# Attention with sixteen heads: the last probability tile of a head joins GpSimd's partial sum by an accumulating transfer instead of by an add

## The chip, the cores and the metric

The kernel runs on one core of a Trainium2 chip. The metric is the device time of one execution in microseconds (us), lower is better. Three runs of the kernel before gave 4175.97, 4178.22 and 4180.62 us.

## What is computed

A transformer block on four sequences of 2048 tokens with 512 channels, all in fp32:

```python
xn = _layernorm(x)
q, k, v = heads of (xn @ q_w.T + q_b) / sqrt(32), xn @ k_w.T + k_b, xn @ v_w.T + v_b   # 16 heads of 32 channels
attn = softmax(q @ k.T)                       # per head 2048 x 2048
ctx = attn @ v
out = x + (ctx @ out_w.T + out_b) + tanh(xn @ weight @ aux_weight1 @ aux_weight2 + bias)
```

With four sequences and sixteen heads there are 64 heads to attend.

## The kernel before

Three stages follow each other: the weights (`build_weights`), the projections (`build_project`) and attention with the output projection (`build_attend`). The first two end near 830 us and the change does not touch them.

**A head in attention.** The scores are held transposed, keys in partitions. A head has 16 tiles (`KT`), each of 128 keys by 2048 queries, that is 128x2048 fp32 or 1 MB. TensorE makes the scores of a tile in four units of 512 queries (`scores`, L942), ScalarE takes the exponential of each unit into the tile (`exps`, L762), and TensorE multiplies the tile with v (`use`, L948) and adds up in `pv_bank`. Between the score units of this head TensorE makes plain scores of a following head (`max_scores`, L926), whose row maxima VectorE takes (L846); that maximum goes into the scores as one more row. TensorE works in pairs of tiles: sixteen score matmuls, then `use` of an earlier pair.

**The denominator.** All 16 tiles of a head also have to be summed over the keys. Elementwise sums of whole tiles are made first, in two places. Tiles 0, 2, 5, 8, 10 and 13 (`CHAINS`) go into `dma_sum`: tile 0 is written there by ScalarE, and the others are added by DMAs that accumulate in SBUF (`join` 1 to 5, L708, issued by GpSimd). The other ten tiles (`POOL_TILES`: 1, 3, 4, 6, 7, 9, 11, 12, 14, 15) are summed in `pool_sum` by nine GpSimd adds (`add` 0 to 8, L697). Then `merge` (L716) adds `pool_sum` onto `dma_sum` by one more accumulating DMA. TensorE multiplies the result with ones (`add_up`, L948 with `dma_sum,ones_att`), ScalarE copies it, VectorE takes the reciprocals in three pieces and GpSimd multiplies (`scale`, L722). Both sums are double-buffered by the head's parity.

**GpSimd's order.** Its instruction stream is written out by hand. In `body(h)`, for i from 0 to 8, it runs `sum_up` of the next head h+1, with the merge of head h behind the first of them and `scale(h)` ahead of the last:

```python
JOIN_AFTER = {1: 2, 3: 3, 5: 4, 7: 5}
# body(h): join1(h+1), add0(h+1), merge(h), add1, join2, add2, add3, join3,
#          add4, add5, join4, add6, add7, join5, scale(h), add8(h+1)
```

A join waits for its tile's exponentials and for the landing of the join before it (`joined`, L702 to L706); join 1 waits also until TensorE has used tile 0. The merge waits for the last add and the last join. All six accumulating DMAs of a head are issued by GpSimd and share one queue, q0.

**TensorE's order.** `add_up(h)` stands behind the score units of tiles 8 and 9 and the use of tiles 6 and 7 of head h+1. It waits for the landing of the merge (`joined`), and everything behind it on TensorE waits with it.

**Buffers.** The probability tiles other than tile 0 rotate through eight buffers (`SLOT`). ScalarE may write a tile when TensorE has used the buffer's former tile and the sum has taken it in: `exps` waits for `pool_added` or for `joined` (L753 to L760). Tile 7 of head h+1 follows tile 15 of head h in its buffer.

Of the kernel before, what the change touches and what calls it, by code (L numbers as in the profile page):

```python
# [8 lines left out]
ALU = mybir.AluOpType  # L9
# [13 lines left out]
DMA = 16  # L23
PRIME = 16


KT = SEQ // P
QT = SEQ // P
QB = SEQ // BLK
ALL_HEADS = BATCH * HEADS  # L30
GROUP = 4
# [3 lines left out]
UNITS = KT * QB  # L35
# [9 lines left out]

CHAINS = [[0, 2, 5, 8, 10, 13]]
MERGE_AFTER = 0
POOL_TILES = [kt for kt in range(KT) if not any(kt in tiles for tiles in CHAINS)]
POOL_ADDS = len(POOL_TILES) - 1
JOINED = len(CHAINS[0]) * DMA  # L50
JOIN_AFTER = {1: 2, 3: 3, 5: 4, 7: 5}
SLOT = {kt: i % 7 for i, kt in enumerate([*range(1, 13), 14, 15])} | {13: 7}
SCALE_ADD = 8
RESULT_TILES = [9, 11]


# [20 lines left out]
def st_place(u):  # L77
    return st_slot(u) % ST_BANKS
# [10 lines left out]
def adds_after(kt):  # L89

    return max(1, POOL_TILES.index(kt))


def tile_before(kt):

    same = [t for t in SLOT if SLOT[t] == SLOT[kt]]
    i = same.index(kt)
    return same[i - 1], int(i == 0)
# [422 lines left out]
def build_attend(nc, dram, out, first):  # L521

    with ExitStack() as own:
        sb = lambda name, shape, dt=F32: own.enter_context(nc.sbuf_tensor(name, shape, dt))
        ps = lambda name, shape: own.enter_context(nc.psum_tensor(name, shape, F32))
        sem = lambda name: own.enter_context(nc.semaphore(name))
# [4 lines left out]
        pool_sum = [sb(f"pool_sum{s}", [P, SEQ]) for s in range(2)]  # L533
# [16 lines left out]
        scores_ready, probs_ready, tile_used = sem("scores_ready"), sem("probs_ready"), sem("tile_used")  # L550
        max_scores_ready, max_scores_read = sem("max_scores_ready"), sem("max_scores_read")
        row_max_ready, turned_ready, max_row_ready = sem("row_max_ready"), sem("max_turned"), sem("max_row_ready")
        join_due, joined = sem("join_due"), [sem("joined0"), sem("joined1")]
        pool_added, sums_ready, recip_ready, context_ready = sem("pool_added"), sem("sums_ready"), sem("recip_ready"), sem("context_ready")
        pv_copied, sums_copied = sem("pv_copied"), sem("sums_copied")
        context_stored = [sem("context_stored0"), sem("context_stored1")]
# [16 lines left out]
        def heads(eng, body, extra=0):  # L573


            with nc.Fori(0, ALL_HEADS // GROUP - 1, engines=[eng.engine], hint_back_edge=True,
                         head_slot={eng.engine: 0}) as i:
                after = [eng.snap(i + 1 + n) for n in range(1 + extra)]
                for r in range(GROUP):
                    body(i * GROUP + r, r, GROUP, *(a * GROUP + (r + 1 - GROUP - n * GROUP) for n, a in enumerate(after)))  # L580
            for r in range(GROUP):
                body(ALL_HEADS - GROUP + r, r, GROUP - 1 - r, *[ALL_HEADS - GROUP + r + 1] * (1 + extra))
# [9 lines left out]
        def tile_at(r, kt):  # L592

            return dma_sum[r % 2] if kt == CHAINS[0][0] else probs[SLOT[kt]]

        def landed(h, j):

            return (h // 2) * JOINED + j * DMA
# [76 lines left out]
        @block.gpsimd  # L675
        def _(pool):
            pool.sem_inc(pool_added, PRIME)
            pool.sem_inc(context_ready, PRIME)
            nc.gpsimd.memset(ident[:], 0.0).then_inc(ident_zero, 1)
            nc.gpsimd.memset(ones[:], 1.0).then_inc(consts_ready, 1)  # L680
            pool.wait_ge(ident_zero, 1)
            nc.gpsimd.affine_select(out=ident[:], in_=ident[:], compare_op=ALU.not_equal, fill=1.0, base=0,
                                    pattern=[[-1, P]], channel_multiplier=1).then_inc(consts_ready, 1)
            for r in range(GROUP):
                pool.wait_ge(consts_ready, 2 + r)
                nc.gpsimd.memset(k_st[r][MROW:MROW + 1, :].bitcast(F32), 1.0).then_inc(consts_ready, 1)

            def add(h, r, i):

                total, kt = pool_sum[r % 2], POOL_TILES[i + 1]  # L690
                if i == 0:
                    pool.wait_ge(sums_ready, PRIME + h - 1)
                pool.wait_ge(probs_ready, PRIME + h * UNITS + QB * (kt + 1))
                one = tile_at(r, POOL_TILES[0]) if i == 0 else total
                if i:
                    pool.wait_ge(pool_added, PRIME + h * POOL_ADDS + i)
                nc.gpsimd.tensor_tensor(total[:], one[:], tile_at(r, kt)[:], ALU.add).then_inc(pool_added, 1)  # L697

            def join(h, r, j):


                pool.wait_ge(probs_ready, PRIME + h * UNITS + QB * (CHAINS[0][j] + 1))  # L702
                if j == 1:
                    pool.wait_ge(tile_used, PRIME + h * KT + CHAINS[0][0] + 1)
                if j > 1 or not (isinstance(h, int) and h < 2):
                    pool.wait_ge(joined[r % 2], landed(h, j - 1))  # L706
                pool.sem_inc(join_due, 1)
                nc.gpsimd.dma_start(dma_sum[r % 2][:], tile_at(r, CHAINS[0][j])[:],  # L708
                                    accum_op=ALU.add).then_inc(joined[r % 2], DMA)

            def merge(h, r):

                pool.wait_ge(pool_added, PRIME + h * POOL_ADDS + POOL_ADDS)
                pool.wait_ge(joined[r % 2], landed(h, len(CHAINS[0]) - 1))
                pool.sem_inc(join_due, 1)
                nc.gpsimd.dma_start(dma_sum[r % 2][:], pool_sum[r % 2][:], accum_op=ALU.add).then_inc(joined[r % 2], DMA)  # L716

            def scale(h, r):
                pool.wait_ge(pv_copied, PRIME + h + 1)
                pool.wait_ge(recip_ready, h * len(RECIPS) + len(RECIPS))  # L720
                pool.wait_ge(context_stored[r % 2], PRIME + (h // 2) * (CTX_DMAS * DMA))
                nc.gpsimd.tensor_tensor(ctx_out[r % 2][:], pv_copy[r % 2][:], ratio[:], ALU.mult).then_inc(context_ready, 1)  # L722

            def sum_up(h, r, i):
                if i == 0:
                    join(h, r, 1)
                add(h, r, i)
                if i in JOIN_AFTER:
                    join(h, r, JOIN_AFTER[i])

            for i in range(POOL_ADDS):
                sum_up(0, 0, i)

            def body(h, r, more, following):
                for i in range(POOL_ADDS):
                    if i == SCALE_ADD:
                        scale(h, r)
                    if more >= 1:
                        sum_up(following, (r + 1) % GROUP, i)
                    if i == MERGE_AFTER:  # L740
                        merge(h, r)

            heads(pool, body)

        @block.scalar
        def _(act):
# [3 lines left out]
            def exps(h, r, kt):  # L750

                for q in range(QB):
                    if q == 0 and kt in SLOT:  # L753
                        old, back = tile_before(kt)
                        act.wait_ge(tile_used, PRIME + h * KT - back * KT + old + 1)
                        if old in POOL_TILES:
                            act.wait_ge(pool_added, PRIME + h * POOL_ADDS - back * POOL_ADDS + adds_after(old))
                        elif old != kt and not (back and isinstance(h, int) and h == 0):
                            before, place = (h - 1, (r + 1) % 2) if back else (h, r % 2)
                            act.wait_ge(joined[place], landed(before, CHAINS[0].index(old)))  # L760
                    act.wait_ge(scores_ready, h * UNITS + kt * QB + q + 1)  # L761
                    nc.scalar.activation(tile_at(r, kt)[:, q * BLK:(q + 1) * BLK],  # L762
                                         st_bank[:, st_place(kt * QB + q)], ACT.Exp,
                                         scale=SCALE).then_inc(probs_ready, 1)
# [24 lines left out]
            for kt in range(CUT):  # L789
                exps(0, 0, kt)  # L790
                if kt in LOAD_AT:
                    load(GROUP - 1, GROUP - 1, LOAD_AT.index(kt))
# [297 lines left out]
```

## Time and profile before

| | |
|---|---|
| Runs | 4175.97, 4178.22, 4180.62 us (median 4178.22) |
| Profiled execution | 4178.57 us, span of the core 4176.8 us |
| TensorE busy | 4086.4 us, 98% |
| GpSimd busy | 3251.6 us, 78% of the whole; 979.66 of 1000 us within attention |
| VectorE, ScalarE busy | 74%, 57% |
| DMA, mean over 16 engines | 0.44 in the projections, 0.82 in attention |
| Granted TensorE clock | 0.99 of full speed |

Busy shares average over stages that have different limits. Attention runs from about 830 to 3990 us. Within it the shares are those of one stretch of 1000 us in the rows below. In the waits, an entry says which instruction waited and what ended the wait. In the timeline, a row is one instruction, or several of one kind merged, with its start, its length and the idle time before it. Times from issue to landing are those of single transfers.

### The profile page before, as it was taken

Reading aid. Unit: us, or ns where it says so; the run is one execution under the profiler, and the core shown is the slowest. Engines: PE = TensorE matmul, PEld = TensorE weight load, DVE = VectorE, ACT = ScalarE, POOL = GpSimd, SP = SyncE. Lnnn points to the kernel's source line nnn. Section 1 sums busy time; section 2 is a strip of 40 time slices with the busy share of each in tenths; the row PEclk is TensorE's granted clock in tenths of the full one; section 3 lists DMA queues with packets and bytes.
Section 4 is the critical chain, followed back from the end, with each engine's and each line's share of the span. In section 5 each row is a group of like instructions: output and inputs, shape, how many; then the busy total and the mean of one; then the engine's idle time right before and its main releaser. Section 6 shows DMA issues by size and latency. Waiting matters only on the chain.

```text
span 4176.8 us, 77708 instructions
## 1 busy us (share of the span) xinstructions
PE 4086.4 (98%) x21216; PEld 2490.0 (60%) x21216; DVE 3110.1 (74%) x5056; ACT 2360.6 (57%) x4517; POOL 3251.6 (78%) x1183
## 2 busy tenths in 40 slices
PE   8999999899999999999999999999999999999989
PEld 6888888655555555555555555555555555555467
DVE  4443334588888888888888888888888888888444
ACT  2221222166666666666666666666666667666621
POOL 1222222279999999999999999999999999999920
PEclk9999999999999999999999999999999999999999
DMA  4444445368788888888888888888888888887777
GB/s 169 163 162 158 151 161 170 132 139 170 166 177 175 179 170 174 171 173 172 175 177 173 175 171 167 172 175 177 176 171 172 173 173 175 176 178 163 167 248 250
DMA packets 246256, 722.11 MB, mean 173 GB/s; under 512 B 87296, under 2 KB 88320, under 8 KB 184448
## 3 DMA queue, kind: packets, MB, share of 16 engines
q0 software_dynamic: 55296, 402.68, 49.8%
q1 hardware_dynamic: 107552, 201.88, 14.2%
q10 hardware_dynamic: 83040, 113.01, 9.7%
q8 instruction: 185, 3.03, 0.3%
q14 instruction: 183, 1.50, 0.1%
HBM read 178.00 MB, written 136.31 MB: 75 GB/s over the span
## 4 chain that ended last, share of the span: by engine, by line
PE 48%; DMA 18%; issue 9%; ACT 3%; POOL 2%; POOLq 0%; DVE 0%; ACTq 0%; SPq 0%; DVEq 0%
PE sm_bank L926 14%; PE st_bank L942 14%; PE pv_bank L948 14%; DMA dma_sum<-pool_sum 10%; DMA dma_sum<-probs 7%; PE sm_bank L235 3%; ACT probs L762 3%; PE sm_bank L948 1%; POOL pool_sum L697 1%; PE st_bank L235 1%; POOL ctx_out L722 1%; POOL dma_sum L708 0%; PE sm_bank L935 0%; ACTq L761 0%; DMA k_stack<-s_k_hi 0%
## 5 line engine op out<-in xcount | busy, mean ns | idle before, releaser
L846 DVE TENSOR_REDUCE part_max<-sm_bank 128x1 f32<-128x512 f32 x4032 | 2450.4, 677 | 413.8 <-PE sm_bank L926 407.4
L697 POOL TENSOR_TENSOR pool_sum<-pool_sum,probs 128x2048 f32<-128x2048 f32 x512 | 2503.2, 4889 | 18.1 <-ACT probs L762 2.2
L762 ACT ACTIVATE probs<-st_bank 128x512 f32<-128x512 f32 x3840 | 1959.3, 614 | 610.5 <-PE st_bank L942 577.7
L926 PE MATMUL sm_bank<-k_stack,q_stack 96*128 96x512 f32 x4032 | 1663.0, 413 | 4.4 <-issue 2.7
L942 PE MATMUL st_bank<-q_stack,k_stack 97*128 97x512 f32 x4096 | 1647.1, 403 | 14.8 <-ACT probs L762 8.5
L926 PEld LDWEIGHTS sm_bank<-k_stack,q_stack 96*128 96x128 f32 x4032 | 767.2, 190 | 558.8 <-DVE part_max L846 339.0
L942 PEld LDWEIGHTS st_bank<-q_stack,k_stack 97*128 97x128 f32 x4096 | 778.6, 190 | 271.4 <-ACT probs L762 127.6
L948 PE MATMUL pv_bank<-probs,v_pair 128*32 128x512 f32 x7680 | 937.6, 603 | 0.0
L948 PEld LDWEIGHTS pv_bank<-probs,v_pair 128*32 128x32 f32 x7680 | 204.9, 109 | 457.3 <-ACT probs L762 264.0
L708 POOL DMA_DIRECT2D dma_sum<-probs x320 | 349.3, 1092 | 80.3 <-ACT probs L762 35.2
L349 POOL TENSOR_TENSOR y_out<-y_out,x_in 128x512 f32<-128x512 f32 x64 | 82.7, 1292 | 385.7 <-ACT y_out L378 379.9
L697 POOL TENSOR_TENSOR pool_sum<-probs 128x2048 f32<-128x2048 f32 x64 | 330.5, 5164 | 0.1
L838 DVE RECIPROCAL ratio<-sum_copy 128x168 f32<-128x168 f32 (+1 forms) x192 | 230.5, 1202 | 42.3 <-ACT sum_copy L769 42.3
L372 ACT ACTIVATE qk_hi<-proj,qk_bias 128x512 fp32r<-128x512 f32 x128 | 88.3, 690 | 271.3 <-PE proj L235 271.3
L431 DVE SCALAR_TENSOR_TENSOR qk_lo<-proj,qk_bias,qk_hi 128x512 fp32r<-128x512 f32 x128 | 96.1, 751 | 194.8 <-ACT qk_hi L372 193.0
L378 ACT ACTIVATE y_out<-y_out 128x512 f32<-128x512 f32 x64 | 40.5, 633 | 333.0 <-DVE y_out L457 333.0
L762 ACT ACTIVATE dma_sum<-st_bank 128x512 f32<-128x512 f32 x256 | 132.5, 602 | 146.5 <-PE st_bank L942 146.5
L235 PE MATMUL proj<-xt_hi,w_hi 128*128 128x512 f32 x512 | 202.9, 396 | 2.2 <-DVEq L461 2.2
L235 PE MATMUL proj<-w_hi,xt_lo 128*128 128x512 f32 x512 | 204.0, 398 | 0.0
L235 PE MATMUL proj<-xt_hi,w_lo 128*128 128x512 f32 x512 | 203.0, 396 | 0.0
L235 PE MATMUL proj<-xt_lo,w_hi 128*128 128x512 f32 x512 | 202.8, 396 | 0.0
L235 PE MATMUL proj<-w_hi,xt_hi 128*128 128x512 f32 x512 | 202.3, 395 | 0.0
(100 smaller groups left out, 2401.6 us busy)
## 6 DMA issues: line engine op xcount, KB each, us to landing
dma_sum<-probs POOLq DMA_DIRECT2D x320, 1024.0 KB, 8.3
dma_sum<-pool_sum POOLq DMA_DIRECT2D x64, 1024.0 KB, 10.3
q_stack<-s_q_hi ACTq DMA_DIRECT2D x122, 256.0 KB, 5.6
k_stack<-s_k_hi ACTq DMA_DIRECT2D x122, 256.0 KB, 4.4
x_in<-in_x SPq DMA_DIRECT2D x16, 1024.0 KB, 7.7
s_q_hi<-qk_hi SPq DMA_DIRECT2D x16, 1024.0 KB, 4.3
s_q_lo<-qk_lo SPq DMA_DIRECT2D x16, 1024.0 KB, 6.5
s_k_hi<-qk_hi SPq DMA_DIRECT2D x16, 1024.0 KB, 4.3
```

The lines of the kernel that those rows point to most:

```text
L235: last = nc.tensor.matmul(out, a(c), b(c), start=(c == 0 and n == 0), stop=(c == CT - 1 and n == 2))
L349: nc.gpsimd.tensor_tensor(y_out[:, j], y_out[:, j], x_in[par][:, j], ALU.add).then_inc(half_y, 1)
L372: nc.scalar.activation(qk_hi[:, t, g], proj[:, u % RING], ACT.Identity, bias=keep["qk_bias"][:, t, g:g + 1]).then_inc(hi_ready, 1)
L431: nc.vector.scalar_tensor_tensor(qk_lo[:, t, g], proj[:, u % RING], keep["qk_bias"][:, t, g:g + 1], qk_hi[:, t, g].bitcast(F32), ALU.add, ...
L697: nc.gpsimd.tensor_tensor(total[:], one[:], tile_at(r, kt)[:], ALU.add).then_inc(pool_added, 1)
L708: nc.gpsimd.dma_start(dma_sum[r % 2][:], tile_at(r, CHAINS[0][j])[:], accum_op=ALU.add).then_inc(joined[r % 2], DMA)
L762: nc.scalar.activation(tile_at(r, kt)[:, q * BLK:(q + 1) * BLK], st_bank[:, st_place(kt * QB + q)], ACT.Exp, scale=SCALE).then_inc(probs_r ...
L838: nc.vector.reciprocal(ratio[:, columns], sum_copy[r % 2][:, columns]).then_inc(recip_ready, 1)
L846: nc.vector.tensor_reduce(part_max[:, k:k + 1], sm_bank[:, sm_place(k)], AX.X, ALU.max).then_inc(max_scores_read, 1)
L926: nc.tensor.matmul(sm_bank[:, sm_place(k)], q_st[r][0:ROWS, q * P:(q + 1) * P], k_st[r][0:ROWS, b * BLK:(b + 1) * BLK], start=True, stop=T ...
L942: nc.tensor.matmul(st_bank[:, st_place(u)], k_st[r][0:ROWS + 1, kt * P:(kt + 1) * P], q_st[r][0:ROWS + 1, q * BLK:(q + 1) * BLK], start=Tr ...
L948: last = nc.tensor.matmul(bank[q * DH:(q + 1) * DH, :], left, right[:, q * BLK:(q + 1) * BLK], start=start, stop=stop)
```

## The change

GpSimd's last add of a head (`add` 8, tile 15) is taken out. In its place tile 15 is added onto `pool_sum` by an accumulating DMA, `top_up`, with semaphores `topped` of its own. It waits until ScalarE has made tile 15 and until the last of the eight adds left is done. `merge` now waits for the landing of that transfer instead of for the last add. `scale(h)` moves out of the loop: it stands ahead of `top_up(h+1)`, the last thing in `body(h)`. ScalarE, before it writes tile 7 of the next head over tile 15, waits for `topped`.

```diff
-POOL_TILES = [kt for kt in range(KT) if not any(kt in tiles for tiles in CHAINS)]
+TOP = KT - 1
+POOL_TILES = [kt for kt in range(TOP) if not any(kt in tiles for tiles in CHAINS)]
...
-SCALE_ADD = 8
...
+        topped = [sem("topped0"), sem("topped1")]
...
+            def top_up(h, r):
+
+                pool.wait_ge(probs_ready, PRIME + h * UNITS + QB * (TOP + 1))
+                pool.wait_ge(pool_added, PRIME + h * POOL_ADDS + POOL_ADDS)
+                pool.sem_inc(join_due, 1)
+                nc.gpsimd.dma_start(pool_sum[r % 2][:], tile_at(r, TOP)[:], accum_op=ALU.add).then_inc(topped[r % 2], DMA)
+
             def merge(h, r):
 
-                pool.wait_ge(pool_added, PRIME + h * POOL_ADDS + POOL_ADDS)
+                pool.wait_ge(topped[r % 2], (h // 2) * DMA + DMA)
                 pool.wait_ge(joined[r % 2], landed(h, len(CHAINS[0]) - 1))
...
             for i in range(POOL_ADDS):
                 sum_up(0, 0, i)
+            top_up(0, 0)
 
             def body(h, r, more, following):
                 for i in range(POOL_ADDS):
-                    if i == SCALE_ADD:
-                        scale(h, r)
                     if more >= 1:
                         sum_up(following, (r + 1) % GROUP, i)
                     if i == MERGE_AFTER:
                         merge(h, r)
+                scale(h, r)
+                if more >= 1:
+                    top_up(following, (r + 1) % GROUP)
...
                         if old in POOL_TILES:
                             act.wait_ge(pool_added, PRIME + h * POOL_ADDS - back * POOL_ADDS + adds_after(old))
+                        elif old == TOP and not (isinstance(h, int) and h == 0):
+                            act.wait_ge(topped[(r + 1) % 2], ((h - 1) // 2) * DMA + DMA)
```

## Rows read from the trace of the kernel before

**Rows 1.** The page: TensorE's share, queue q0, the merge's landing (median).

```profile
PE 4086.4 (98%) x21216; PEld 2490.0 (60%) x21216; DVE 3110.1 (74%) x5056; ACT 2360.6 (57%) x4517; POOL 3251.6 (78%) x1183
...
q0 software_dynamic: 55296, 402.68, 49.8%
...
dma_sum<-pool_sum POOLq DMA_DIRECT2D x64, 1024.0 KB, 10.3
```

**Rows 2.** Busy time per window: stretch, PE, PEld, DVE, ACT, POOL, clock, DMA share, GB/s.

```profile
2000.00:3000.00 1000.00, 987.74 (x5430) 546.81 (x5431) 869.43 (x1418) 691.20 (x1354) 979.66 (x328) 1.00 0.82 172
```

**Rows 3.** Waits of the whole span: who waited for whom, us, times, longest.

```profile
PEld sm_bank L948 <- DMA dma_sum<-pool_sum: 76.4, 58, 2.3
...
POOL dma_sum L708 <- ACT probs L762: 35.2, 46, 2.2
...
POOL dma_sum L708 <- DMA dma_sum<-probs: 12.7, 15, 1.3
```

**Rows 4.** Timeline of TensorE: start of `add_up` in heads 1, 60, 56 and 57.

```profile
971.22 0.61 PE L948 MATMUL sm_bank<-dma_sum,ones_att 128*32 128x512 f32 x4
...
3852.48 0.61 PE L948 MATMUL sm_bank<-dma_sum,ones_att 128*32 128x512 f32 x4
...
3656.93 0.61 PE L948 MATMUL sm_bank<-dma_sum,ones_att 128*32 128x512 f32 x4
...
3705.08 0.61 PE L948 MATMUL sm_bank<-dma_sum,ones_att 128*32 128x512 f32 x4
```

**Rows 5.** Timeline of GpSimd over one head, from a join 1 to the next add 8.

```profile
2029.89 1.18 POOL L708 DMA_DIRECT2D dma_sum<-probs  x1
...
2035.03 1.51 POOL L716 DMA_DIRECT2D dma_sum<-pool_sum  x1
2035.77 5.38 POOL L697 TENSOR_TENSOR pool_sum<-pool_sum,probs 128x2048 f32<-128x2048 f32 x1
2040.30 1.69 POOL L708 DMA_DIRECT2D dma_sum<-probs  x1
2041.24 10.02 POOL L697 TENSOR_TENSOR pool_sum<-pool_sum,probs 128x2048 f32<-128x2048 f32 x2
2052.25 0.88 POOL L708 DMA_DIRECT2D dma_sum<-probs  x1 [0.99 <-ACT probs L762]
...
2062.40 0.84 POOL L708 DMA_DIRECT2D dma_sum<-probs  x1
...
2072.47 0.89 POOL L708 DMA_DIRECT2D dma_sum<-probs  x1
2073.09 1.59 POOL L722 TENSOR_TENSOR ctx_out<-pv_copy,ratio 128x512 f32<-128x512 f32 x1
2074.35 4.86 POOL L697 TENSOR_TENSOR pool_sum<-pool_sum,probs 128x2048 f32<-128x2048 f32 x1
```

**Rows 6.** Single transfers issued at 2029.89, 2035.03, 2040.30, 2072.47: KB, us to landing.

```profile
dma_sum<-probs POOLq DMA_DIRECT2D x1, 1024.0 KB, 7.4
...
dma_sum<-pool_sum POOLq DMA_DIRECT2D x1, 1024.0 KB, 10.9
...
dma_sum<-probs POOLq DMA_DIRECT2D x1, 1024.0 KB, 11.4
...
dma_sum<-probs POOLq DMA_DIRECT2D x1, 1024.0 KB, 7.2
```

**Rows 7.** Timeline of TensorE, same head: use of tile 0, then `add_up`.

```profile
2025.17 1.06 PE L948 MATMUL pv_bank<-dma_sum,v_pair 128*32 128x512 f32 x8
...
2046.01 1.07 PE L948 MATMUL sm_bank<-dma_sum,ones_att 128*32 128x512 f32 x8 [1.11 <-DMA dma_sum<-pool_sum]
```

**Rows 8.** Busy time per window around an idle stretch of TensorE, columns as rows 2.

```profile
870.66:873.35 2.69, 0.00 (x1) 0.01 (x1) 0.00 (x0) 0.00 (x0) 2.69 (x2) 0.89 0.14 34
873.35:876.00 2.65, 2.65 (x6) 2.14 (x7) 1.50 (x3) 1.15 (x2) 2.65 (x2) 0.50 0.75 148
876.00:880.00 4.00, 4.00 (x11) 2.84 (x9) 3.35 (x6) 2.73 (x6) 2.64 (x1) 0.55 0.92 170
```

## The prediction

> **What bounds the kernel now.** The page comes first: TensorE is busy 98% of the span [rows 1]. The windows come second, since the shares are averages over stages: within attention TensorE is busy 987.74 of 1000 us and GpSimd 979.66 [rows 2], so two engines have hardly any idle time and either could set the pace. The waits come third. TensorE's weight load for `add_up` waited 58 times for the merge to land, 76.4 us in all, about once a head; GpSimd's own waits are 35.2 and 12.7 us [rows 3]. So TensorE is last to be served at one place only, `add_up`, and what it waits for is the end of GpSimd's chain: adds, merge, landing.
>
> What that wait costs is read from the starts of `add_up`. Between heads 1 and 60 lie 2881.26 us, which is 48.83 us a head. Between heads 56 and 57 neither shows a wait before it, and they are 48.15 us apart [rows 4]. So TensorE alone needs 48.15 us, and the wait costs 0.68 us a head. That is the most that the change can gain if it makes the merge early and nothing else is late: 0.68 x 61 = 41 us.
>
> GpSimd's round is read from the timeline [rows 5]: from merge to the end of `scale` 2074.35 - 2035.03 = 39.32 us, of which 0.99 are a wait. Add 8 follows (4.5 us: the last add before a join, as 2040.30 - 2035.77 = 4.53), then 2035.03 - 2029.89 = 5.14 for join 1 and add 0. Sum without the wait: 38.33 + 4.53 + 5.14 = 48.0. GpSimd has as good as no slack against 48.15.
>
> **What the change removes.** One add a head, 4.53 us of GpSimd. It puts in an issue, 0.62 us (2073.09 - 2072.47) [rows 5]. GpSimd's work falls to 48.0 - 4.5 + 0.6 = 44.1 us a head, 4 us below TensorE's 48.15. By this count alone the merge would come up to 4 us earlier and the wait of 0.68 us would go. `scale` keeps its 1.26 us and now only stands ahead of a DMA issue rather than an add; at nothing, as its operands are ready well before it (it follows join 5 without a gap in rows 5).
>
> **What the change adds: a seventh transfer on q0, and a wait for it in the middle of GpSimd's stream.** Behind the waiting merge stand add 1, join 2 and all further adds of the head, and behind the landing of the merge stands TensorE. So the landing time of `top_up` becomes a term in GpSimd's own round. It has to be priced.
>
> How transfers on q0 follow each other: join 1 is alone and lands 7.4 us after issue, at 2037.3. The merge, issued at 2035.03, takes 10.9 and lands at 2045.9. Join 2, issued at 2040.30, takes 11.4 and lands at 2051.7, 5.8 behind the merge [rows 5, 6]. One issued with nothing ahead lands in 7.2 us [rows 6]. That is a first-in, first-out queue: each transfer waits for the one ahead and then takes 5 to 6 us of all engines. The page gives the floor: 49.8% of 4176.8 us over 384 transfers is 5.42 us each [rows 1]. Six a head are 32.5 us, 0.67 of 48.83; the DMA share is 0.82 [rows 2], so other queues take 0.16, and a transfer among them takes 5.42 / 0.84 = 6.4. I take 5.8 for a queued transfer, this head's spacing and near the middle of 5.4 and 6.4. A queue with seven of them also has fewer gaps left: 0.82 + 5.42 / 48.83 = 0.93 of the DMA engines' time at the old pace.
>
> GpSimd wakes 0.5 us after a landing: join 2 landed at 2051.7 and join 3 went out at 2052.25 [rows 5, 6]. (The row names ScalarE as releaser, but join 3 also waits for this landing and that fits.)
>
> The new round, from merge issue (time 0) to the next merge issue:
> - merge, add 1, join 2, add 2, add 3: 2041.24 + 10.02 - 2035.03 = 16.23 us [rows 5].
> - join 3 must wait for join 2 to land. In front of it in the queue now stand join 1 and the merge, and join 1 itself could only start when `top_up` had landed (at -0.5). Join 1 lands at -0.5 + 5.8 = 5.3. The merge lands 8.05 behind it (median 10.3 from issue [rows 1], issued 5.14 behind a join 1 that lands in 7.4), at 13.35. Join 2 lands 5.8 later, 19.1, and the wake makes it 19.6. Wait: 19.6 - 16.2 = 3.3 us, against 0.99 now.
> - join 3 to join 4: 10.15; join 4 to join 5: 10.07; join 5 and `scale`: 2074.35 - 2072.47 = 1.88 [rows 5].
> - `top_up` is issued 1.88 us behind join 5. Join 5 lands 7.2 to 7.4 after its own issue, so 5.5 after that of `top_up`; `top_up` lands one transfer later, 11.3; the wake makes 11.8 us. In that time GpSimd has join 1 and add 0 to do, 5.8 us with the issue of `top_up`, and then it stands still.
>
> Sum: 16.2 + 3.3 + 10.15 + 10.07 + 1.88 + 11.8 = 53.4 us a round. GpSimd's work became shorter, its round longer, because 11.8 us of a transfer took the place of 4.5 + 5.1 us of adding, and join 3 waits more.
>
> Could TensorE be later still? The merge lands at 13.35, `add_up` follows there. Tile 0 of the next head was used 2026.2 (start 2025.17, 1.06 long), 18.7 us before the 2044.9 at which `add_up` would have run without its wait of 1.11 [rows 7]. So the next join 1 is allowed at 13.35 + 48.15 - 18.7 = 42.8, GpSimd reaches it at 42.2; add 0 ends at 48, and the merge waits until 53.4 anyhow. TensorE is ready for the next `add_up` at 61.5, the merge lands at 66.8: it waits some 5 us a head. ScalarE's tile 7, which now waits for `topped`, comes about one and a half pairs of tiles before `add_up`, a pair being 48.15 / 8 = 6.0 us, so at 52.5 against a landing of 52.9: a fraction of a us, hidden in those 5.
>
> **Bounds of the unknown term.** Low: a queued transfer takes only the 5.42 floor everywhere, so join 3 waits for nothing and `top_up` lands at 7.2 - 1.88 + 5.42 + 0.5 = 11.2. The round is 16.2 + 0 + 10.15 + 10.07 + 1.88 + 11.2 = 49.5, which is 0.7 x 61 = 43 us slower. High: 6.4 everywhere; join 3 waits 4.6, `top_up` takes 7.4 - 1.88 + 6.4 + 0.5 = 12.4; 55.3 us, 395 us slower. I take the middle, since the 5.8 and the 8.05 are what this queue shows when it is filled. A gain is possible only if `top_up` does not queue (first rival).
>
> The Trainium skill (DMA: Bandwidth & Descriptors, Anatomy of one DMA — SWDGE (gpsimd) path) fits a transfer as 2.0 us plus bytes over 436 GB/s, which is an estimate of 4.4 us for 1 MB, of which 2.4 would be moving. By that page `top_up` behind join 5 would land in about 5 us, no join would wait, and TensorE's 48.15 would set the pace: the first rival's time. This trace disagrees: 7.2 us for one alone and 5.42 us of engine time.
>
> **The rivals.**
> 1. The top-up is hidden, faster. If its landing and the wait at join 3 together stayed under 48.15 - 38.3 = 9.8 us, TensorE would bind and the 0.68 us go: 4178.6 - 41 = 4137. For it: GpSimd's 4 us of freed time, and a lone transfer's 7.2 + 0.5 would do. Against it: join 5 is always issued only 1.88 us ahead, so the top-up is never alone. Chance 0.06.
> 2. Queue spacing at its floor: rounds of 49.5 to 51, 4220 to 4310. For it: the single pair of 5.8 is near the floor. Against: 8.05 for the merge. Chance 0.09.
> 3. TensorE's clock as well. After TensorE had stood idle for 2.69 us its granted clock was 0.50 and 0.55 for the next 6.7 us [rows 8], the 1.2 GHz level; that is 3.3 us of work lost. With an idle stretch of 5 us a head this would come once a head. One such loss leaves TensorE at 61.5 + 3.3 = 64.8, still ahead of 66.8, so it is hidden; a second one in the head would make the round about 55.5 or more: above 4535. Chance 0.05. The Trainium skill (TensorE: Matmul & The Clock Gate, HAM oscillation — how this bites in real kernels) describes the same pattern, a DMA wait in every tile that lets the clock fall every time; the rows agree for one gap, and by the sum it costs nothing here.
> 4. The change does not do what it says: the issue of `top_up` or join 1 with two transfers outstanding blocks GpSimd until one lands (issue rows already grow from 0.88 to 1.69 us when the queue is filled [rows 5]). It would take join 1 to about 47 and leave the merge where it is: no change in the round; counted with the forecast.
> 5. Nothing measurable, 4170 to 4187: gain and loss cancel near a round of 48.8. Chance 0.02.
>
> **How the numbers follow.** The profiled execution took 4178.57 us, the median of the runs is 4178.22, the same within 0.01%. 61 rounds have all transfers and loads; each gets 53.4 - 48.83 = 4.57 us longer: 279 us. The chain starts with empty queues, so I take one round's excess off, 4.6 us, an estimate. The last two heads have no loads beside them and `add_up` of the last stands behind other matmuls: nothing added. 4178.6 + 279 - 4.6 = 4453 us. Forecast (rounds of 51 to 54.9, 4310 to 4545) has 0.78. The range 4320 to 4530 leaves out the first two rivals, the clock and the edges. A measurement of this kernel tells about 0.2% from no change. Slower by over 0.2%: 0.78 + 0.09 + 0.05 = 0.92; within: 0.02; faster: 0.06.
>
> **What would show it.** After the change: starts of `add_up` 53 us apart; a wait of GpSimd's merge for DMA `pool_sum<-probs` of 4 to 6 us in every head, near 300 us in all, that was not there; `top_up` landing 11 to 12 us after issue; join 3 waiting some 3 us for DMA; TensorE's wait for the merge near 5 us a head and its busy share near 0.9; the granted clock below 1 for a stretch after each `add_up`. It is wrong if `top_up` lands in under 8 us, or if the waits of the merge are near nothing.

## The result and the profile after

The changed kernel takes 4473.97 us (median of four runs, 4470.83 to 4483.35) against 4179.42 for the kernel before: a ratio of 1.0712, 95% interval 1.0699 to 1.0726. The forecast was 4453 us, with a range of 4320 to 4530. The profiled execution took 4476.29 us, its span 4474.5, so 297.7 us more than the one before.

The page: busy time of the engines, q0's packets, bytes and share, and the median time from issue to landing of the three kinds of transfers on it.

```profile
PE 4187.7 (94%) x21216; PEld 2545.4 (57%) x21216; DVE 3123.0 (70%) x5056; ACT 2376.7 (53%) x4517; POOL 3013.6 (67%) x1183
...
q0 software_dynamic: 64512, 469.79, 54.1%
...
dma_sum<-probs POOLq DMA_DIRECT2D x320, 1024.0 KB, 8.8
pool_sum<-probs POOLq DMA_DIRECT2D x64, 1024.0 KB, 11.8
dma_sum<-pool_sum POOLq DMA_DIRECT2D x64, 1024.0 KB, 12.4
```

Against [rows 1] GpSimd is busy 238 us less, as the change meant, and nothing became shorter by it: the merge lands 12.4 us after its issue instead of 10.3, and the new transfer takes 11.8. The windows of the same stretch as [rows 2]:

```profile
2000.00:3000.00 1000.00, 931.58 (x4965) 514.27 (x4964) 797.74 (x1295) 635.79 (x1237) 822.38 (x300) 0.97 0.86 177
```

GpSimd's busy time fell from 979.66 to 822.38 of 1000 us, TensorE's from 987.74 to 931.58. No engine is full any more. The waits of the whole span, which answer to [rows 3] (L725 is the merge, L710 a join, L961 with `sm_bank` is `add_up`):

```profile
POOL dma_sum L725 <- DMA pool_sum<-probs: 221.9, 51, 12.3
PEld sm_bank L961 <- DMA dma_sum<-pool_sum: 211.3, 55, 7.5
...
POOL dma_sum L710 <- PE pv_bank L961: 189.7, 49, 22.3
...
PE sm_bank L961 <- DMA dma_sum<-pool_sum: 160.0, 54, 7.0
...
POOL dma_sum L710 <- ACT probs L775: 91.6, 48, 3.8
POOL dma_sum L710 <- DMA dma_sum<-probs: 85.5, 61, 4.3
```

The joins now wait for TensorE too: it is join 1, which may go only when tile 0 has been used. In the round below it cost nothing, since the merge behind it waits longer for the top-up.

One round of GpSimd, which answers to [rows 5], from a merge to the next:

```profile
2035.11 0.88 POOL L725 DMA_DIRECT2D dma_sum<-pool_sum  x1 [3.88 <-DMA pool_sum<-probs]
2035.73 4.88 POOL L699 TENSOR_TENSOR pool_sum<-pool_sum,probs 128x2048 f32<-128x2048 f32 x1
2041.37 0.88 POOL L710 DMA_DIRECT2D dma_sum<-probs  x1 [0.76 <-DMA dma_sum<-probs]
2041.99 9.48 POOL L699 TENSOR_TENSOR pool_sum<-pool_sum,probs 128x2048 f32<-128x2048 f32 x2
2053.41 0.88 POOL L710 DMA_DIRECT2D dma_sum<-probs  x1 [1.94 <-DMA dma_sum<-probs]
...
2063.54 0.88 POOL L710 DMA_DIRECT2D dma_sum<-probs  x1
...
2073.64 0.88 POOL L710 DMA_DIRECT2D dma_sum<-probs  x1
2074.25 1.59 POOL L731 TENSOR_TENSOR ctx_out<-pv_copy,ratio 128x512 f32<-128x512 f32 x1
2075.49 1.19 POOL L718 DMA_DIRECT2D pool_sum<-probs  x1
2077.19 0.88 POOL L710 DMA_DIRECT2D dma_sum<-probs  x1 [0.50 <-issue]
2077.76 4.92 POOL L699 TENSOR_TENSOR pool_sum<-probs 128x2048 f32<-128x2048 f32 x1
2088.53 0.88 POOL L725 DMA_DIRECT2D dma_sum<-pool_sum  x1 [5.85 <-DMA pool_sum<-probs]
```

The round is 53.42 us. The single transfers of its end, issued at 2073.64, 2075.49, 2077.19, 2088.53 and 2094.64, take to their landings:

```profile
dma_sum<-probs POOLq DMA_DIRECT2D x1, 1024.0 KB, 7.5
pool_sum<-probs POOLq DMA_DIRECT2D x1, 1024.0 KB, 12.4
dma_sum<-probs POOLq DMA_DIRECT2D x1, 1024.0 KB, 16.9
dma_sum<-pool_sum POOLq DMA_DIRECT2D x1, 1024.0 KB, 11.2
dma_sum<-probs POOLq DMA_DIRECT2D x1, 1024.0 KB, 11.4
```

Issue plus time gives landings at 2081.1, 2087.9, 2094.1, 2099.7 and 2106.0: five transfers one behind the other, 5.6 to 6.8 us apart. Before, four followed each other like that: join 5, join 1, the merge and join 2. Join 5 of the kernel before stands ahead of the join 1 that [rows 5] begin with; here are its issue and its time to landing.

```profile
2023.49 0.86 POOL L708 DMA_DIRECT2D dma_sum<-probs  x1
...
dma_sum<-probs POOLq DMA_DIRECT2D x1, 1024.0 KB, 7.6
```

It lands at 2031.1, and join 1 had gone out at 2029.89. In all 58 heads of the kernel before between 1000 and 3850 us join 1 goes out before join 5 has landed.

**What closes the round.** In 56 of these 58 heads join 3 goes out 0.57 us after the landing of join 2, and so it does in all 52 heads of the same stretch in the changed kernel, also where a row names ScalarE as what ended the wait (`L708 <- ACT probs`, `L710 <- ACT probs`). So nearly all of these waits are waits for the queue. A round can then be added up along the queue, from join 3 to the next join 3. The means in us, with the first two experiments beside them:

| | before | changed | e1 | e2 |
|---|---|---|---|---|
| join 3 to join 5 (GpSimd's adds) | 20.38 | 20.30 | 20.36 | 20.28 |
| join 5, issue to landing | 7.58 | 7.58 | 7.57 | 7.51 |
| seventh transfer, landing after that of join 5 | none | 6.27 | none | 6.35 |
| join 1, landing after the one ahead | 6.71 | 6.42 | 6.45 | 6.13 |
| merge, the same | 7.52 | 6.73 | 7.20 | 6.88 |
| join 2, the same | 6.05 | 5.60 | 6.63 | 5.79 |
| landing of join 2 to join 3 | 0.58 | 0.57 | 0.57 | 0.56 |
| round | 48.82 | 53.47 | 48.78 | 53.50 |

The seventh transfer puts 6.27 us into this loop, and the other terms lose 1.6 us together.

**Where the 297.7 us are.** The starts of `add_up` in heads 1 and 59 of the changed kernel, and in head 63, the last; then heads 59 and 63 of the kernel before (head 1 of it is in [rows 4]).

```profile
978.37 1.08 PE L961 MATMUL sm_bank<-dma_sum,ones_att 128*32 128x512 f32 x4 [3.82 <-DMA dma_sum<-pool_sum]
...
4084.26 1.08 PE L961 MATMUL sm_bank<-dma_sum,ones_att 128*32 128x512 f32 x4 [4.91 <-DMA dma_sum<-pool_sum]
...
4297.59 1.08 PE L961 MATMUL sm_bank<-dma_sum,ones_att 128*32 128x512 f32 x4 [7.03 <-DMA dma_sum<-pool_sum]
```

```profile
3803.06 0.64 PE L948 MATMUL sm_bank<-dma_sum,ones_att 128*32 128x512 f32 x4 [0.78 <-DMA dma_sum<-pool_sum]
...
4001.64 0.64 PE L948 MATMUL sm_bank<-dma_sum,ones_att 128*32 128x512 f32 x4
```

58 rounds take 3105.89 us, 53.55 each, against 2831.84 us, 48.82 each: 274.0 us. The last four heads take 213.3 instead of 198.6 us: 14.7. The rest, 9 us, lies ahead of head 1 (7.2) and behind the last (1.7).

### The profile page after: what moved, and what is told of

Same layout as the page of the kernel before. It is cut to its first block and busy times, and to the rows that moved or that the text cites. A ratio compares the mean times of both kernels' runs of the same rounds, so it can differ in the third digit from the quotient of the medians.

```text
span 4474.5 us, 77768 instructions
## 1 busy us (share of the span) xinstructions
PE 4187.7 (94%) x21216; PEld 2545.4 (57%) x21216; DVE 3123.0 (70%) x5056; ACT 2376.7 (53%) x4517; POOL 3013.6 (67%) x1183
## 5 line engine op out<-in xcount | busy, mean ns | idle before, releaser
L699 POOL TENSOR_TENSOR pool_sum<-pool_sum,probs 128x2048 f32<-128x2048 f32 x448 | 2132.6, 4760 | 18.1 <-ACT probs L775 2.3
L955 PE MATMUL st_bank<-q_stack,k_stack 97*128 97x512 f32 x4096 | 1687.4, 413 | 76.6 <-ACT probs L775 56.9
L939 PE MATMUL sm_bank<-k_stack,q_stack 96*128 96x512 f32 x4032 | 1701.0, 423 | 4.6 <-issue 4.2
L939 PEld LDWEIGHTS sm_bank<-k_stack,q_stack 96*128 96x128 f32 x4032 | 791.4, 196 | 582.6 <-DVE part_max L859 296.9
L955 PEld LDWEIGHTS st_bank<-q_stack,k_stack 97*128 97x128 f32 x4096 | 802.5, 196 | 350.9 <-ACT probs L775 180.8
L961 PE MATMUL pv_bank<-probs,v_pair 128*32 128x512 f32 x7680 | 944.6, 607 | 0.0
L710 POOL DMA_DIRECT2D dma_sum<-probs x320 | 287.6, 899 | 380.7 <-PE pv_bank L961 189.7
L961 PEld LDWEIGHTS pv_bank<-probs,v_pair 128*32 128x32 f32 x7680 | 205.3, 110 | 457.1 <-ACT probs L775 248.0
L961 PE MATMUL sm_bank<-dma_sum,ones_att 128*32 128x512 f32 x512 | 88.3, 769 | 160.0 <-DMA dma_sum<-pool_sum 160.0
L725 POOL DMA_DIRECT2D dma_sum<-pool_sum x64 | 58.5, 914 | 231.9 <-DMA pool_sum<-probs 221.9
L782 ACT ACTIVATE sum_copy<-sm_bank 128x512 f32<-128x512 f32 x64 | 38.3, 598 | 329.9 <-PE sm_bank L961 329.9
## 6 DMA issues: line engine op xcount, KB each, us to landing
pool_sum<-probs POOLq DMA_DIRECT2D x64, 1024.0 KB, 11.8
dma_sum<-pool_sum POOLq DMA_DIRECT2D x64, 1024.0 KB, 12.4
```

Source lines behind the costliest of these rows:

```text
L939: nc.tensor.matmul(sm_bank[:, sm_place(k)], q_st[r][0:ROWS, q * P:(q + 1) * P], k_st[r][0:ROWS, b * BLK:(b + 1) * BLK], start=True, stop=T ...
L955: nc.tensor.matmul(st_bank[:, st_place(u)], k_st[r][0:ROWS + 1, kt * P:(kt + 1) * P], q_st[r][0:ROWS + 1, q * BLK:(q + 1) * BLK], start=Tr ...
L961: last = nc.tensor.matmul(bank[q * DH:(q + 1) * DH, :], left, right[:, q * BLK:(q + 1) * BLK], start=start, stop=stop)
```

## The experiments

Two theories were set against each other. Theory Q: the seventh transfer lengthens a run of queued transfers, and join 3 cannot go before the last of them has landed. Theory W: GpSimd stands still at the merge until the top-up has landed. The forecast's sum held both. In some of these kernels the denominator is incomplete; their expectations say so.

**The transfer left out** (e1_no_transfer).

```diff
-                pool.wait_ge(topped[r % 2], (h // 2) * DMA + DMA)
+                pool.wait_ge(pool_added, PRIME + h * POOL_ADDS + POOL_ADDS)
...
-                if more >= 1:
-                    top_up(following, (r + 1) % GROUP)
```

> The changed kernel without top_up: eight adds, six transfers, the merge waits for the last add as before; tile 15 is left out of the denominator. Theory Q (the seventh transfer fills queue q0) and theory W (GpSimd stands still at the merge until the top-up has landed) both say that the 4 us of freed GpSimd time put the merge ahead of TensorE: rounds of 48.15 us, about 4137 us. If GpSimd's freed time were worth nothing by itself, it would stay at 4179 us.

Measured: 4174.36 us, ratio 0.9984 (0.9974 to 0.9994). Both theories missed: taking an add of 4.5 us off GpSimd is worth 4 us in all, not 41. Its waits:

```profile
POOL dma_sum L710 <- DMA dma_sum<-probs: 134.0, 50, 4.3
...
POOL dma_sum L710 <- PE pv_bank L956: 120.7, 53, 23.0
...
POOL dma_sum L710 <- ACT probs L770: 91.6, 41, 4.6
...
PEld sm_bank L956 <- DMA dma_sum<-pool_sum: 60.7, 41, 3.5
...
PE sm_bank L956 <- DMA dma_sum<-pool_sum: 26.6, 26, 2.6
```

The freed time turned into waits of the joins: for landings from 12.7 to 134.0 us, in the rows that name ScalarE from 35.2 to 91.6 [rows 3], and for TensorE 120.7. TensorE still waits for the merge. The merge's median landing is 12.4 us in this kernel, against 10.3 [rows 1]: it was issued some 2 us earlier and landed no earlier, since join 1 was still ahead of it. Join 3 goes 0.57 us after the landing of join 2 in all 58 heads, and the same four transfers stand in the loop of the table. So the loop through q0 set the round of the kernel before already. GpSimd's work, 48.0 us, was only 0.8 us shorter.

**The transfer kept, the wait taken away** (e2_no_wait). The same megabyte is added onto a spare buffer, so that nothing makes the merge wait for it.

```diff
-                nc.gpsimd.dma_start(pool_sum[r % 2][:], tile_at(r, TOP)[:], accum_op=ALU.add).then_inc(topped[r % 2], DMA)
+                nc.gpsimd.dma_start(spare[:], tile_at(r, TOP)[:], accum_op=ALU.add).then_inc(topped[r % 2], DMA)
...
-                pool.wait_ge(topped[r % 2], (h // 2) * DMA + DMA)
+                pool.wait_ge(pool_added, PRIME + h * POOL_ADDS + POOL_ADDS)
```

> The changed kernel with the seventh transfer at its place and of its size, but into a spare buffer, so that the merge waits only for the last add; tile 15 is left out of the denominator. Theory W: the wait of the merge is the cost, so it goes: 4137 to 4200 us. Theory Q: join 5, the spare transfer, join 1, merge and join 2 still run one behind the other, 5 x 6.2 us, and join 3 waits for join 2: rounds of 53 us as in the changed kernel, 4430 to 4480 us, with the wait moved from the merge to join 3 (about 9 us instead of 2).

Measured: 4468.84 us, ratio 1.0678 (1.066 to 1.0697), 5 us under the changed kernel. The waits of GpSimd and of TensorE:

```profile
POOL dma_sum L714 <- DMA dma_sum<-probs: 321.9, 74, 7.2
...
PEld sm_bank L967 <- DMA dma_sum<-pool_sum: 192.2, 56, 6.3
...
POOL dma_sum L714 <- ACT probs L781: 79.1, 38, 3.8
```

There is no wait at the merge any more, and the joins wait 401.0 us in the two rows for landings and for ScalarE instead of 177.1. The 221.9 us moved from one place to the other. Theory W falls as the cause of this cost, Q holds: the sum along the queue gives the same round as in the changed kernel. With the first experiment, in which only the transfer was missing, this brackets the cause: 294 us come with the transfer, and 5 more with the wait for it while the queue is as full as this.

**The merge one add later** (e3_merge_later): the order is add 1, merge, join 2.

```diff
-MERGE_AFTER = 0
+MERGE_AFTER = 1
...
                 add(h, r, i)
+                if between is not None:
+                    merge(*between)
                 if i in JOIN_AFTER:
```

> The changed kernel with the merge issued one add later (after add 1, ahead of join 2), so that GpSimd adds while the top-up is under way. Theory W: the 4 to 6 us of standing still are filled with 4.5 us of adding: rounds of about 49 us, 4190 to 4240 us. Theory Q: the queue holds top-up and join 1 until 4.6 us after the merge was issued anyhow, and join 3 still waits for join 2: no change, 4440 to 4490 us, with the wait at the merge shorter and that at join 3 longer by the same.

Measured: 4497.58 us, ratio 1.0752 (1.0728 to 1.0776). The wait at the merge fell from 221.9 us to 36.9, the joins' waits for landings rose from 85.5 to 266.3. It is 24 us slower than the changed kernel and 8 us above Q's range: the round is 54.06 us, and in 10 of 52 heads join 1 had landed before the merge went out, so that the queue stood empty. The moved wait agrees with Q, but the test is weaker than it was meant to be: join 2 also waits for join 1, which stands behind the top-up in the queue, so theory W should have forecast less gain than it did.

**The loads moved away from the run** (e4_after_loads). ScalarE's queue issues the 256 KB loads of a later head behind certain tiles.

```diff
-LOAD_AT = [6, 7, 9, 10, 12, 13, 15]
+LOAD_AT = [1, 2, 3, 11, 13, 14, 15]
```

> The changed kernel with the loads of a following head issued behind tiles 1, 2, 3, 11, 13, 14, 15 instead of 6, 7, 9, 10, 12, 13, 15, away from the five transfers that follow each other without a gap. Theory Q with a queue whose data time binds: three or four 256 KB loads of 0.8 us leave that stretch, rounds 2 to 3 us shorter, 4290 to 4360 us. Theory W, or a queue bound by fixed delays: under 1 us a round, 4420 to 4480 us.

Measured: 4405.57 us, ratio 1.0533 (1.0515 to 1.0551): 68 us less, 1.2 us a round. The direction is Q's, the size half of what it said. The rest shows in where the loads went: the top-up now takes 13.8 us (median), since join 5 and the top-up run beside them. And another chain closes the round: join 3 goes right behind the landing of join 2 in only 8 of 54 heads, but the merge goes 0.65 us after the landing of the top-up in 52. Here the wait of theory W sets the pace, at 52.4 us a round.

```profile
POOL dma_sum L725 <- DMA pool_sum<-probs: 385.5, 60, 12.3
```

**Loads away from join 5 and the top-up as well** (e9_after_loads_mid).

```diff
-LOAD_AT = [6, 7, 9, 10, 12, 13, 15]
+LOAD_AT = [0, 10, 11, 12, 13, 14, 15]
```

> The changed kernel with the loads behind tiles 0 and 10 to 15, so that none falls beside join 5 and the top-up either (with the loads behind tiles 1, 2, 3 these two took 6.5 to 7.2 us each instead of 5.4 to 5.8). Theory Q (data time of the run join 5, top-up, join 1, merge, join 2 sets the round): another 1 to 2 us a round, 4290 to 4350 us. If the run is at its floor already: 4395 to 4415 us as with the first placing.

Measured: 4342.86 us, ratio 1.0386 (1.0369 to 1.0404), in the range that Q gave. From the issue of join 5 to the landing of join 2 the changed kernel takes 32.6 us and this one 29.7 (means), 2.9 us less with three loads fewer beside the run; `add_up` comes every 51.39 us instead of 53.55, 2.2 us less. Most of the run's shortening passes into the round, but not all, since the queue no longer closes the round in most heads. Join 3 goes right behind the landing of join 2 in only 20 of 55; the merge waits for the top-up in some, and join 1 for TensorE in nearly all:

```profile
POOL dma_sum L710 <- PE pv_bank L961: 269.1, 56, 23.1
...
POOL dma_sum L725 <- DMA pool_sum<-probs: 149.2, 38, 12.3
...
POOL dma_sum L710 <- DMA dma_sum<-probs: 9.6, 12, 1.4
```

**Loads moved and the wait taken away** (e10_no_wait_loads): e2's edit with e4's `LOAD_AT`.

> The seventh transfer into the spare buffer, no wait for it at the merge, and the loads behind tiles 1, 2, 3, 11, 13, 14, 15; tile 15 is left out of the denominator. With the loads moved, the changed kernel shows its standing still at the merge alone (6 us a round) and none at join 3. Theory W for that case: without the wait it falls by most of that, to 4140 to 4250 us. Theory Q: join 2 lands at the same place in the queue's order, the wait moves to join 3, 4380 to 4415 us.

Measured: 4382.84 us, ratio 1.0479 (1.0461 to 1.0496). Against e4's 4405.57 the wait is worth 23 us here, more than the 5 us of the first pair; theory W would have had 150 or more. In the trace the joins again take it over, and join 2 goes 0.57 us after the landing of join 1 in 53 of 54 heads:

```profile
POOL dma_sum L714 <- DMA dma_sum<-probs: 308.5, 61, 6.8
```

So with the loads moved each of the two chains was seen closing the round by itself, that of theory W in e4 (52.4 us) and that of the queue here (52.2).

**The same loads moved in the kernel before** (e5_before_loads): all nine adds, six transfers, the whole denominator, `LOAD_AT = [1, 2, 3, 11, 13, 14, 15]` and nothing else.

> The kernel before with only the loads moved (issued behind tiles 1, 2, 3, 11, 13, 14, 15), away from join 1, merge and join 2. Theory Q: the 256 KB loads between them made the merge land late; it lands 0.7 to 1.5 us earlier, TensorE's wait of 0.68 us a round nearly goes: 4140 to 4155 us. If the loads do not matter to the queue: 4179 us.

Measured: 4147.29 us, ratio 0.9922 (0.9908 to 0.9935). It is faster than both kernels. TensorE waits for the merge in two heads instead of 58, and it is busy 996.89 of 1000 us:

```profile
PEld sm_bank L948 <- DMA dma_sum<-pool_sum: 3.2, 2, 2.2
...
2000.00:3000.00 1000.00, 996.89 (x5498) 551.32 (x5496) 877.31 (x1431) 699.84 (x1369) 990.37 (x334) 1.00 0.82 176
```

**Eight adds, no transfer, loads moved** (e7_no_transfer_loads): e1 with e5's `LOAD_AT`.

> Eight adds, six transfers, tile 15 left out of the denominator as in the run without the transfer, and the loads moved. In that run GpSimd issued the merge earlier and it landed no earlier, since the queue was still busy. Theory Q: with the loads out of the way the merge lands before TensorE asks in nearly every head: rounds of 48.15 us, 4135 to 4145 us. If the freed GpSimd time is lost elsewhere: about 4174 us again.

Measured: 4140.94 us, ratio 0.9908 (0.989 to 0.9926). This is the gain that the forecast's first rival had in mind, 41 us, and it comes only once the loads are out of the queue's way and without the seventh transfer. Of the 40 us, 33 come without the missing add (e5). GpSimd's 4.5 us a head are worth 6 us in all, roughly: the runs of each of the two kernels spread over 4 to 5 us.

**A seventh transfer at another place** (e8_gap_transfer). The kernel before with all nine adds; one megabyte more is moved into a spare buffer behind add 6.

```diff
                 if i in JOIN_AFTER:
                     join(h, r, JOIN_AFTER[i])
+                if i == 6:
+                    if not (isinstance(h, int) and h == 0):
+                        pool.wait_ge(spared[(r + 1) % 2], ((h - 1) // 2) * DMA + DMA)
+                    pool.sem_inc(join_due, 1)
+                    nc.gpsimd.dma_start(spare[:], tile_at(r, 12)[:], accum_op=ALU.add).then_inc(spared[r % 2], DMA)
```

> The kernel before, all nine adds and the whole denominator, with a seventh transfer of 1 MB from tile 12 into a spare buffer, issued after add 6, where the queue is empty. Theory Q as a matter of place (a transfer costs where it lengthens a run of queued ones): it lands before join 5 goes out; only its issue of 0.6 us on GpSimd counts, rounds of 48.8 to 49.6 us, 4179 to 4230 us. If the bytes alone cost (a queue that is full on average): 53 us a round as after the change, 4400 to 4480 us.

Measured: 4269.91 us, ratio 1.0211 (1.0193 to 1.023), between the two. The place decides two thirds of the cost, 89 us instead of 295, but the transfer is not free, and the expectation that it meets an empty queue was wrong. In all 56 heads between 1000 and 3850 us it goes out before join 4 has landed, and join 5 before it has landed itself. The kernel before leaves q0 empty for 4.0 us a round, in three pieces (0.6 before join 3, 1.4 before join 4, 2.0 before join 5, means), and a transfer takes 5.4 [rows 1]: there is no gap that holds one. The timeline at a merge:

```profile
2117.94 2.11 POOL L720 DMA_DIRECT2D dma_sum<-pool_sum  x1
2119.30 5.37 POOL L701 TENSOR_TENSOR pool_sum<-pool_sum,probs 128x2048 f32<-128x2048 f32 x1
```

The merge's issue now keeps GpSimd for 1.36 us (2119.30 - 2117.94) where it was 0.74 [rows 5], and GpSimd's round without waits is 48.8 us (50.69 from this merge to the next, less waits of 1.11 and 0.74), over TensorE's 48.15. The remaining waits, 1.6 us a round, nearly all at join 3, had two possible sources, so the loads were moved here too (e11_gap_transfer_loads).

> The kernel before with the seventh transfer into a spare buffer behind add 6, and the loads behind tiles 1, 2, 3, 11, 13, 14, 15. With the loads at their old places GpSimd's round of that kernel held 48.8 us of work and issues and 1.6 us of waits for landings. If those waits come from the loads beside the run of queued transfers, they go: rounds of 48.8 to 49.3 us, 4175 to 4210 us. If seven transfers a head are too many bytes wherever they stand, the waits stay: 4250 to 4280 us.

Measured: 4242.12 us, ratio 1.0157 (1.014 to 1.0174), in neither forecast. Joins 2 to 5 hardly wait any more (1.1 us in all between 1000 and 3800 us), but the merge now waits for join 5, which stands behind the seventh transfer and runs beside the moved loads (the row is of the same stretch):

```profile
POOL dma_sum L720 <- DMA dma_sum<-probs: 51.9, 32, 2.8
```

Against the kernel with six transfers and the same loads (e5) a seventh at this place costs 95 us, against the kernel before with the old loads 89: the same 1.5 us a head. About half is GpSimd's own work, 48.8 us instead of 48.0. The other half is the queue, and the traces show where: in e8 join 3 goes 0.57 us after the landing of join 2 in 49 of 56 heads, and in e11 the merge goes 0.57 us after that of join 5 in all 56 and waits 1.0 us a round for it.

**TensorE kept busy while it waits** (e6_fill).

```diff
+                if more >= 2:
+                    r1 = (r + 1) % GROUP
+                    for _ in range(14):
+                        nc.tensor.matmul(sum_bank, q_st[r1][0:ROWS, 0:P], k_st[r1][0:ROWS, 0:BLK], start=True, stop=True)
                 pe.wait_ge(joined[r % 2], landed(h, len(CHAINS[0])))
```

> The changed kernel with 14 matmuls of scores more (3.3 us of TensorE, their result is overwritten) ahead of add_up's wait, so that TensorE is busy for most of the time it waits for the merge. If the fall of the granted clock after each wait costs time at the end (heads in which TensorE is late by itself), the clock stays near 1 and the time falls from 4474 to 4400 to 4455 us. If the clock's loss is hidden in the wait, as forecast: 4465 to 4500 us.

Measured: 4477.9 us, ratio 1.0712 (1.0693 to 1.0731), the changed kernel's. The mean granted clock rose from 0.966 to 0.987, TensorE's wait for the merge fell from 160.0 to 22.1 us, and the time stayed. In the changed kernel TensorE is idle before one `add_up` (first row), and the clock is at its 1.2 GHz level soon after it (second row):

```profile
2418.85:2422.60 3.75, 0.00 (x0) 0.00 (x0) 0.00 (x0) 0.00 (x0) 3.67 (x2) 1.00 1.03 240
...
2424.10:2427.40 3.30, 3.30 (x10) 2.49 (x9) 2.77 (x4) 2.36 (x5) 0.25 (x1) 0.50 0.44 89
```

The trace has 41 such falls between 1000 and 4080 us, 205 us in all at half speed, for some 58 heads; with the additional matmuls there are 9. What that takes is hidden in TensorE's slack, and 3.3 us of additional matmuls a head were free too.

## Why the prediction was right, and which of its steps were not

**The round.** Forecast 53.4 us, measured 53.55. By its terms, in the round shown above: merge to the end of add 3 16.36 (forecast 16.2), of which 0.76 is a wait of join 2 for join 1 that the sum did not have, and the two adds were 0.5 shorter; join 3's wait 1.94 (3.3); join 3 to join 4 10.13 and to join 5 10.10 (10.15, 10.07); join 5 to top-up 1.85 (1.88); top-up to the next merge 13.04 (11.8). The last is the largest miss: the top-up landed in 12.4 us here and in 11.8 in the median, against 11.3. The errors at join 3 and at the top-up cancel, which is luck. Two prices of the queue were off in opposite ways too: the merge was taken to land 8.05 us behind join 1 and does so 6.73 behind it (mean), the top-up and join 1 were given 5.8 and took 6.3 and 6.4.

**What makes the round long.** The sum was right and the weight that the text gave its terms was not. It said that the round grew "because 11.8 us of a transfer took the place of 4.5 + 5.1 us of adding, and join 3 waits more", and named the wait in the middle of GpSimd's stream as what the change adds. e2 took that wait away and won 5 us. The queue closes the round by itself: join 5, top-up, join 1, merge and join 2 one behind the other, and join 3 behind the last, 53.5 us with or without the wait at the merge. The chain through that wait, without the waits at joins 2 and 3 (0.85 and 2.09 us a round in the mean), would take about 50.5 us in the changed kernel, an estimate; it closes the round only where the run is shorter, as in e4. The forecast had the queue as a term (join 3 waits for join 2) and did not ask what that term would be if the wait were gone. For the time it made no difference; for anyone who wants to mend the kernel it does.

**What GpSimd's freed time is worth.** The first step failed here: "by this count alone the merge would come up to 4 us earlier and the wait of 0.68 us would go". In e1 it was worth 4 us of 41. The premise behind it was the reading "join 1 is alone". It had join 5 ahead of it in every head, so the run of transfers that ends in join 2 began before GpSimd's last add was over, and taking that add out could not start it earlier. The forecast had even seen that join 3 goes 0.5 us after the landing of join 2, and took it for one wait of 0.99 us; it was what set the round. TensorE waited for the merge because q0 delivered it late, with loads of the next head between (e5 and e7). The chance of a gain (0.06) was set low for another reason, the top-up's place behind join 5, which held.

**The size.** The forecast gave 274 us, the profiled execution has 297.7. That the 58 rounds up to head 59 alone make 274.0 is a coincidence. By the forecast's own count these rounds had 265 (58 x 4.57), 9 too few, as a round grew by 4.72 us. Ahead of head 1 one round's excess and the deduction of 4.6 us for the start left nothing, and 7.2 came. The last four rounds had 9 (two rounds and "nothing added") and took 14.7, and the end 1.7. The last `add_up` now waits 7.03 us, where other matmuls used to cover the merge.

**The signs it named.** The starts of `add_up` and the landing of the top-up came as said. The merge waited 221.9 us for the top-up, not near 300, in 51 heads and not in every one. One reason is join 1: the forecast had it held by TensorE for 0.6 us, and it waits 2.5 us a round in the mean, which shortens the wait at the merge behind it and costs nothing. TensorE's weight load for `add_up` waited 3.8 us a time and not near 5.

**The clock.** It fell as that rival said, though in two heads of three and not in every one (41 falls for some 58 heads, mean 0.966 against 0.99), and the price was rightly nil: e6 shows that it costs nothing.

**A change that does nothing, or blocks.** Join 1 issued behind join 5 and the top-up took 0.88 us (2077.19): two transfers outstanding do not block GpSimd.

**The page of the Trainium skill** (DMA: Bandwidth & Descriptors, Anatomy of one DMA — SWDGE (gpsimd) path) would have had an estimate of 4.4 us for a transfer, about 5 for the top-up, and a gain. The changed kernel's trace has 7.5 us for a transfer with an empty queue and 11.8 for the top-up; measurement decides.

## What to carry to other kernels

Before work is moved from an engine to a DMA queue, write down the queue's own round as for an engine: how many transfers follow each other without a gap, and who must wait for the last of them. An engine that is busy 98% does not hold the kernel if its result then passes through a queue that is late anyhow; the landing time of a transfer with and without something ahead of it tells, and small loads that nobody waits for can be what makes it late. Where an instruction waits for two things, do not go by the name of the releaser alone: if it starts at the same distance from one landing in every head, that landing is what it waits for. When two chains of nearly the same length close a loop, taking the shorter away shows next to nothing, so each has to be taken out by an experiment of its own.

## What the runs showed of the hardware that was not expected

- Accumulating 1 MB transfers within SBUF on one queue land 5.6 us (join 2 of the changed kernel) to 7.5 us (merge of the kernel before) apart in the mean when queued. With nothing ahead they take 7.6 us (join 5) to 8.8 us (join 3) from issue to landing in the kernel before. A join goes out 0.57 us after the landing that it waits for.
- A 256 KB load from HBM beside such a run costs it about 1 us, an estimate: with three loads fewer beside it (e9) join 1, merge and join 2 take 15.9 us instead of 18.8 in the changed kernel.
- GpSimd's issue of a transfer, to its next instruction, takes 0.62 us with the queue empty, 0.74 and 0.94 us in [rows 5] with one transfer under way, and 1.36 us at the merge of e8 (median) with one under way as well. It is not the number of transfers: with two under way join 1 of the changed kernel takes 0.57 us. What lengthens it is open.
